# Low-frequency attention of a two-layer kernel: exponentials with bias and row sums on ScalarE, straight from the score bank, and four buffers of probabilities

## The reference, cut to what matters

```python
scores = jnp.einsum('bhqd,bhkd->bhqk', q, kk) / np.float32(np.sqrt(HD))
scores = jnp.where(mask[None, None], scores, jnp.finfo(scores.dtype).min)
p = jax.nn.softmax(scores, axis=-1)
o = jnp.einsum('bhqk,bhkd->bhqd', p, v)
...
A_r = _block_causal_attention(X_low.real, q_w, k_w, v_w, o_w, k)
A_i = _block_causal_attention(X_low.imag, q_w, k_w, v_w, o_w, k)
...
A_low_fused = alpha * A_low + (1.0 - alpha) * X_low
Y_hat = jnp.concatenate([A_low_fused, A_high], axis=2)
Y = jnp.fft.irfft(Y_hat, n=C, axis=2)
```

## Time and profile before

| | before |
|---|---|
| median of 3 runs | 1240.88 us |
| the profiled execution's own time | 1238.01 us |
| its span, first to last instruction | 1236.2 us |
| PE busy | 1137.5 us (92%) |
| DVE busy | 839.0 us (68%) |
| ACT busy | 806.7 us (65%) |
| POOL busy | 29.0 us (2%) |
| mean granted clock of PE | 0.965 |

### The profile page before, as it was taken

How to read it: one execution, slowest core, us unless ns; L and a number is a source line. 1 busy time by engine, 2 the same in 40 slices (tenths; PEclk the granted TensorE clock), 3 DMA queues, 4 the chain that set the end, 5 groups by cost and what they waited for, 6 DMA issues and landing times.

```text
span 1236.2 us, 21816 instructions
## 1 busy us (share of the span) xinstructions
PE 1137.5 (92%) x9020; PEld 639.6 (52%) x9020; DVE 839.0 (68%) x1180; ACT 806.7 (65%) x1439; POOL 29.0 (2%) x73
## 2 busy tenths in 40 slices
PE   4874899979899999999999999999999599999998
PEld 3533688842443333333333333333334379797887
DVE  3848533348989999999999999999940621222222
ACT  2434534334259999999999999999998553434442
POOL 0002000000000000000000000000000000000000
PEclk9876999978999999999999999999999899999999
DMA  9000000000000000000000000000000000000000
GB/s 386 12 1 0 1 1 0 1 1 0 1 2 2 2 2 2 2 2 2 2 2 2 2 2 2 2 2 2 2 2 2 0 1 1 10 1 8 0 8 8
DMA packets 5431, 14.84 MB, mean 12 GB/s; under 512 B 352, under 2 KB 4576, under 8 KB 4832
## 3 DMA queue, kind: packets, MB, share of 16 engines
q1 hardware_dynamic: 5056, 10.84, 2.3%
q10 hardware_dynamic: 288, 2.76, 0.5%
HBM read 12.29 MB, written 1.05 MB: 11 GB/s over the span
## 4 chain that ended last, share of the span: by engine, by line
DVE 49%; PE 45%; ACT 3%; issue 1%; DMA 1%; SPq 0%; DVEq 0%; ACTq 0%
DVE mx L1264 41%; PE ps L984 9%; PE ps L715 6%; PE ps L716 5%; PE ps L717 5%; PE ps L864 3%; PE ps L836 3%; PE ps L805 1%; PE ps L781 1%; PE ps L752 1%; PE ps L965 1%; DMA x<-x_in 1%; DVE Qs L1252 1%; PE ps L845 1%; DVE z L1036 1%
## 5 line engine op out<-in xcount | busy, mean ns | idle before, releaser
L1264 DVE TENSOR_REDUCE mx<-ps 128x2 f32<-128x1024 f32 x512 | 587.5, 1215 | 13.8 <-PE ps L805 13.1
L528 ACT ACTIVATE probs<-ps 128x512 f32<-128x512 f32 x1024 | 540.3, 598 | 56.1 <-PE ps L864 48.1
L864 PE MATMUL ps<-Qb,Ks 32*128 32x512 f32 x1024 | 327.5, 495 | 0.5 <-ACT probs L528 0.4
L836 PE MATMUL ps<-probs,V 128*16 128x256 f32 x4096 | 320.1, 385 | 7.2 <-ACT U L522 7.2
L805 PE MATMUL ps<-Ks,Qb 32*128 32x512 f32 x1024 | 257.0, 498 | 8.0 <-DVE mx L1264 5.0
L864 PEld LDWEIGHTS ps<-Qb,Ks 32*128 32x128 f32 x1024 | 149.2, 181 | 213.6 <-issue 121.3
L575 ACT ACTIVATE eh<-ps,MW 128x512 f32<-128x512 f32 x128 | 87.5, 689 | 83.4 <-PE ps L717 82.9
L836 PEld LDWEIGHTS ps<-probs,V 128*16 128x16 f32 x4096 | 67.1, 94 | 133.9 <-issue 78.2
L805 PEld LDWEIGHTS ps<-Ks,Qb 32*128 32x128 f32 x1024 | 95.3, 182 | 46.8 <-DVE mx L1264 31.0
L984 PEld LDWEIGHTS ps<-MW,eh 128*128 128x128 f32 x1024 | 118.3, 192 | 2.4
L984 PE MATMUL ps<-MW,eh 128*128 128x128 f32 x1024 | 119.2, 275 | 0.0
(11 more groups left out here) (218 smaller groups left out, 1096.6 us busy)
## 6 DMA issues: line engine op xcount, KB each, us to landing
MW<-moe_in SPq DMA_DIRECT2D x1, 4454.0 KB, 24.2
FW<-ffn_in SPq DMA_DIRECT2D x1, 2824.5 KB, 12.4
SW<-spectral_in ACTq DMA_DIRECT2D x1, 1479.5 KB, 9.7
DW<-mods_in ACTq DMA_DIRECT2D x1, 1219.0 KB, 6.3
x<-x_in SPq DMA_DIRECT2D x4, 256.0 KB, 10.8
out<-x SPq DMA_DIRECT2D x4, 256.0 KB, 2.3
AW<-attn_in SPq DMA_DIRECT2D x1, 836.5 KB, 13.9
Qb<-mT SPq DMA_DIRECT2D x32, 8.0 KB
```

The costliest lines, as they stand in the source:

```text
L528: act.activation(probs[:, 4 * (s % 4) + g, :], score(n), ACT.Exp, scale=SCALE1) \
L836: last = pe.matmul(ps[32 * g:32 * g + VW, 6, queries], V[:, kt, col:col + VW], probs[:, 4 * (s % 4) + g, queries], start=(kt == 0 and half ...
L864: pe.matmul(score(n), Ks[rows, hg, kt * P:kt * P + P], Qb[rows, hg, :], start=True, stop=True).then_inc(sem.st_ready, 1)
L1264: dve.tensor_reduce(mx[:, k // 16 % 2, k % 16 // 4, k % 4, 2 * pair:2 * pair + 2], ps[:, at:at + 2, :], AX, ALU.max).then_inc(sem.bank_rea ...
```

## The change

The subtraction on DVE goes. DVE now only multiplies the maximum by -1/8 (`sneg`, 128x4), and ACT reads the scores from the bank itself: four exponentials per group, one for each head, each with that head's column of `sneg` as bias and with its row sum written to `ssum`. The row sum on DVE goes too. `Pn` and the small tensors have four buffers. A score bank is now free when the exponentials of its group are done (before, when the subtraction was). DVE's maxima run two groups ahead of the rest of its work instead of one, and ACT's exponentials run two ahead as well, issued between PT(i) and OT(i).

```diff
-                Pn = sb("Pn", [P, 2, G4, P], where=spectral)
+                Pn = sb("Pn", [P, 4, G4, P], where=spectral)
@@
             def low_exp(i):
-                act.wait_ge(sem.s_sub, i + 1)
-                act.activation(Pn[:, i % 2, :, :], Pn[:, i % 2, :, :], ACT.Exp, scale=float(HD) ** -0.5) \
-                   .then_inc(sem.s_exp, 1)
+                act.wait_ge(sem.s_neg, i + 1)
+                if due(i - 3):
+                    act.wait_ge(sem.pT_ready, i - 3)
+                for b in range(G4):
+                    act.activation(Pn[:, i % 4, b, :], ps[:, low_bank[i % 4], b * P:b * P + P], ACT.Exp,
+                                   bias=sneg[:, i % 4, b:b + 1], scale=float(HD) ** -0.5,
+                                   accum_out=ssum[:, i % 4, b:b + 1]).then_inc(sem.s_exp, 1)
 
             low_exp(0)
+            low_exp(1)
             for i, (ri, j) in enumerate(groups):
-                if i + 1 < len(groups):
-                    low_exp(i + 1)
                 act.wait_ge(sem.pT_ready, i + 1)
                 act.activation(PT[:, i % 2, :], bank(2 + i % 2), ACT.Copy).then_inc(sem.pT_copied, 1)
+                if i + 2 < len(groups):
+                    low_exp(i + 2)
                 act.wait_ge(sem.o_ready, i + 1)
@@
                 if due(i - 3):
-                    pe.wait_ge(sem.s_sub, i - 3)
+                    pe.wait_ge(sem.s_exp, 4 * (i - 3))
@@
-                    last = pe.transpose(ps[:, 2 + i % 2, b * P:b * P + P], Pn[:, i % 2, b, :], ident)
+                    last = pe.transpose(ps[:, 2 + i % 2, b * P:b * P + P], Pn[:, i % 4, b, :], ident)
@@
             def low_top(i):
-                p = i % 2
-                s4 = bank(low_bank[i % 4]).rearrange("p (b n) -> p b n", b=G4)
+                p = i % 4
+                s4 = bank(low_bank[p]).rearrange("p (b n) -> p b n", b=G4)
                 dve.wait_ge(sem.s_ready, i + 1)
-                if due(i - 1):
-                    dve.wait_ge(sem.pT_ready, i - 1)
                 dve.tensor_reduce(smax[:, p, :], s4, AX, ALU.max).then_inc(sem.s_max, 1)
                 dve.wait_ge(sem.s_max, i + 1)
-                dve.tensor_tensor(Pn[:, p, :, :], s4, four(smax[:, p, :]), ALU.subtract).then_inc(sem.s_sub, 1)
+                if due(i - 3):
+                    dve.wait_ge(sem.s_exp, 4 * (i - 3))
+                dve.tensor_scalar(sneg[:, p, :], smax[:, p, :], -float(HD) ** -0.5, None, ALU.mult).then_inc(sem.s_neg, 1)
 
             low_top(0)
+            low_top(1)
             for i in range(len(groups)):
-                p = i % 2
-                if i + 1 < len(groups):
-                    low_top(i + 1)
+                p = i % 4
+                if i + 2 < len(groups):
+                    low_top(i + 2)
                 taps(conv[10 + i:11 + i])
-                dve.wait_ge(sem.s_exp, i + 1)
-                dve.tensor_reduce(ssum[:, p, :], Pn[:, p, :, :], AX, ALU.add).then_inc(sem.s_sum, 1)
-                dve.wait_ge(sem.s_sum, i + 1)
+                dve.wait_ge(sem.s_exp, 4 * (i + 1))
                 dve.reciprocal(srcp[:, p, :], ssum[:, p, :]).then_inc(sem.s_rcp, 1)
```

## The result

The changed kernel takes 1225.24 us (median of 4, 1223.92 to 1226.05), the kernel before 1240.01 (median of 4, 1238.28 to 1240.94): a ratio of 0.9889, interval 0.9857 to 0.9921. It is 14.8 us faster. The forecast was 1230.7 with a range from 1226.5 to 1237.5: the sign and the ring of waits were right, the size was not, and the time lies under the range.

A forecast was written before the change was run, and what follows sets the result against it. No engine is full; a ring of waits through DVE and PE bounds the first layer's low-frequency attention. Stage 8.85 us shorter plus 1.4 in the projection, 10.2 off the 1240.9 median, gave 1230.7 us; range 1226.5 to 1237.5.

The forecast's parts named there:

- The ring: First layer's low-frequency attention: a chain of waits through DVE and PE, 4.86 us per group of four heads.
- PE's own 3.06 us per group: PE's transposes, next scores and values product of one group, expected to set the pace in groups 0 to 3.
- T(0) at 49.1: PE's transposes of the first head group start at 49.1 us, 0.7 us later than before.
- The exponentials at 1.85 us: ACT's four 128x128 exponentials with row sums per group, priced 4 x (0.26 + 0.20), between bounds 1.15 and 2.28 us.
- The projection: Output projection behind the attention stage: 5.1 us taken, the middle between 6.49 and 3.69, a gain of 1.4 us.
- clock rival: PE runs at 1.2 GHz for some of the denser attention stretch, leaving a gain of 4: 1236.5 us, chance 14%.
- The lower end of the range: Attention stage with exponentials at 1.15 us and projection at 3.7: gain 12.9, 1228 us; the range reaches to 1226.5.
- The stretch behind: Work after the attention stage, to 125 us, clock at 0.68: pattern shifts with the start, 2 us allowed either way.
- no change: Later clock gives the shorter stage back, or ACT takes near 3.4 us per exponential group: 1241 us, chance 6%.
- slower: In ACT's queue each row sum stops the engine; at 1.1 us per small exponential, 1247 us; chance 3%.

The follow-up runs named there:

- E3: Kernel before with four probability buffers, maxima and exponentials two groups ahead, exponentials issued ahead of the second ACT copy, old arithmetic kept: 1228.90 us.
- E4: Changed kernel with two probability buffers, maxima and exponentials one group ahead as before; the new arithmetic stays: 1230.35 us.
- E9: Changed kernel with each group's exponentials put back behind ACT's second copy; four buffers and the new arithmetic stay: 1231.13 us.
- E6: Changed kernel with each small exponential and its sum issued twice, the first into a scratch tile: 1230.42 us.
- E7: Kernel before with PE's waits in the eight groups filled by products of the identity into an unused bank: 1234.17 us.
- E5: Changed kernel with the row sum back on DVE, the four exponentials writing no sum: 1225.79 us.
- E1: Kernel before, unchanged, run once more for a second profile: 1236.82 us.
- E10: Changed kernel with five products of constants on PE in its wait ahead of the first group's scores: 1227.98 us.
- E11: Changed kernel with PE fillers ahead of the transposes of Y (five), the second normalisation's transposes (seven) and the gated network (two): 1222.54 us.
- E8: Changed kernel with next transposes ahead of values products in the last groups, seven fillers ahead of the second normalisation's transposes and seven ahead of the gated network: 1227.41 us.

## Why the forecast missed

By its own steps:

- **The ring.** Right: PE's own 3.06 us per group was measured as 3.0, ACT took over from T(4), no scaling on DVE held up T(1) to T(3), and no wait for the transposes was left. E3, E4 and E9 show how it divides: by the medians the new arithmetic is worth some 4 us on top of the rest (E3), the place of the exponentials some 6 (E9), and either half alone breaks the ring.
- **T(0) at 49.1.** It came at 47.87, 1.2 us earlier. I had S(2) done at 45.97, its time at the lower clock in the one profile of before, and it was done at 44.91: 1.1 of the 1.2 us are the clock of the start, which E6 and E7 show to be a draw. T(0) to T(1) I had as 3.6 us, partly at the lower clock; it was 3.0: 0.6 us, nearly all the clock. Over the next three turns another 0.2, which is my 3.06 against 3.00.
- **The exponentials at 1.85 us.** They take 1.5. The second instruction that I added is there and as long as I said, but it overlaps as the others do; I gave the overlap to the exponentials and denied it to the reads. From T(4) to the end of OT(7) it was 10.4 us instead of 11.5: 1.1 us, of which 0.9 are the two groups of exponentials in that chain (1.40 each instead of 1.85, since they overlap the copies beside them too). E6 shows that the term is on the path. The 1.27 us that the prediction worked out from the figures of the Trainium skill (ScalarE: Activation LUTs, section What ACT_TABLE_LOAD costs) is an estimate for four without sums; E5 has 1.14, so the trace is 10% below it.
- **The projection.** I took the middle of its two levels, 5.1 us. It was 3.72: 1.4 us.

These make 4.5 us, and 10.2 + 4.5 = 14.7. The other 0.9 us between 1230.7 and 1225.2 is the starting point: I subtracted from a median of 1240.9, and with the fourth run it is 1240.0. About 3 of the 4.5 us, two thirds (1.1 + 0.5 + 1.4), are PE's clock. **The step that failed is the clock**: the sum carried the levels of one profile of before into the new schedule, or split the difference, and my clock rival only let it eat the gain. The runs show the other direction. In both profiles of before the clock was low in S(7), behind the waits; in both of the changed kernel and in E7, which fills those waits and leaves the ring as slow as it was, S(7) ran at full clock, and E7 is 6.9 us faster. My argument said as much for the projection ("more densely") and then priced it at half. Part of it was luck: the level at the start and in the projection of before are draws, and E1, with its projection at 3.72 us, would have given a stage of 45.2 us to start from instead of 49.4. The lower end of the range had the same fault: it took the cheapest exponentials and the full clock in the projection but kept the slow start. With a fast start as well the stage would end 1.8 us earlier, near 1226.2, and the 1.5 us that the range allowed below that would have held the time.

- **The stretch behind**, with 2 us allowed either way, was 0.6 us longer. Its draws are real: 1146.0 to 1150.2 us over the profiles that have no fillers behind the stage.
- **The rivals.** Clock rival, no change and slower all failed on the side on which they stood. E10's profile shows that the clock rival is possible: PE ran at the lower clock from T(0) to V(1) in a stage as dense as the changed one, 3.1 us.

Open: what sets the level of the clock at S(1), and at T(0) in E10, in one execution and not in the next; and why the network's first products stayed slow behind two products of constants (E11) and not behind seven (E8).

## What to carry to other kernels

A removed wait on PE can be worth more than its length, since PE may also run faster behind it (S(7) here, 2.08 us against 1.16): price the following products at both levels of the clock, and put the better one into the range on the gain's side. Do not take one profile's clock for the kernel's. The three runs known at the forecast spread over 1.8 us and hid it; 17 runs spread over 12. In an in-order queue the place of a new instruction (here 6 us between ahead of OT and behind it) can matter more than its cost.

## What the runs showed of the hardware

- A row sum on ACT runs as a second instruction, ACTIVATION_READ_ACCUMULATOR, of 0.19 to 0.22 us, overlapped: it adds some 0.09 us to the distance of 128x128 exponentials (0.34 against 0.26).
- Useless products on PE made the kernel before 6.9 us faster (E7). In the changed one they came with 2.7 us less (E11) and with 2.7 us more (E10, where two of six runs were no slower). Seven of them in front of ready data held PE up for 3.2 us (E8).
- The kernel before spreads over 12 us. In two executions of it the same 16 products of the projection took 3.72 and 6.49 us, and 16 others ahead of the stage 5.89 and 3.69 us.
- A wait of PE of 1.48 us ahead of T(0) was followed by full clock in both profiles of the changed kernel and by the lower clock in E10: the wait ahead of them alone does not tell the level of the products.
